# ScalarE's inverse norm placed in front of the first two gelus, with fewer table changes

## The reference, cut to what matters

```python
def attn_layer(x, Wqkv, qs, ksc, Wo):      # 16 heads of 64, windows of 32 tokens
    q, k, v = split(x @ Wqkv)
    q = l2norm(q) * qs
    k = l2norm(k) * ksc
    q, k = rotary(q, scale), rotary(k, 1 / scale)
    return local_attention(q, k, v) @ Wo

def ffn_layer(x, g, bln, W1, b1, W2, b2):  # 128 -> 2 x 341 -> 128
    xn = layernorm(x) * g + bln
    a, gate = split(xn @ W1 + b1)
    return a * gelu(gate) @ W2 + b2

for i in range(6):
    x = attn_layer(shift_tokens(x), ...) + x
    x = ffn_layer(shift_tokens(x), ...) + x
# whole: x += 0.5 * stack(layernorm(x)); x += retention(layernorm(x)); x += 0.5 * stack(layernorm(x))
```

## Time and profile before

| what | value |
|---|---|
| time, median of 3 runs | 3483.53 us (3481.82 to 3486.94) |
| the profiled execution | 3483.61 us |
| its span, first to last instruction | 3481.8 us |
| TensorE busy | 3337.9 us (96%) |
| VectorE busy | 2858.4 us (82%) |
| ScalarE busy | 2433.7 us (70%) |
| GpSimd busy | 2342.3 us (67%) |
| mean granted TensorE clock | 0.985 |

### The profile page before, as it was taken

The page is one execution under the profiler, slowest core; times in us unless marked ns, Lnnn a source line. Parts: engine busy times, 40 slices in busy tenths (PEclk is TensorE's granted clock), DMA queues, the critical chain, the costliest instruction groups (busy, mean ns, idle before and its releaser), DMA issues.

```text
span 3481.8 us, 123144 instructions
## 1 busy us (share of the span) xinstructions
PE 3337.9 (96%) x51660; PEld 1871.0 (54%) x51660; DVE 2858.4 (82%) x6052; ACT 2433.7 (70%) x4133; POOL 2342.3 (67%) x2188
## 2 busy tenths in 40 slices
PE   6999999999999999999788999999999999999996
PEld 3555555555555555555354555555555555555553
DVE  7888888888888888886468888888888888888883
ACT  3677777777777777777425777777777777777775
POOL 5777777777776777775137777777777777677771
PEclk8999999999999999999899999999999999999999
DMA  2001001001001001000100000000010000000000
GB/s 84 12 15 46 12 14 49 12 14 48 12 15 48 12 14 36 10 13 20 39 1 24 14 24 22 17 24 22 12 29 22 12 28 23 12 28 10 12 5 13
DMA packets 49223, 76.64 MB, mean 22 GB/s; under 512 B 7072, under 2 KB 37024, under 8 KB 47136
## 3 DMA queue, kind: packets, MB, share of 16 engines
q1 hardware_dynamic: 48672, 68.76, 6.3%
HBM read 61.39 MB, written 7.34 MB: 20 GB/s over the span
## 4 chain that ended last, share of the span: by engine, by line
PE 51%; POOL 22%; issue 15%; DVE 10%; ACT 1%; POOLq 0%; DMA 0%; SPq 0%; DVEq 0%; ACTq 0%
PE QA L835 10%; PE VS L899 10%; POOL QN L345 8%; POOL QN L352 8%; PE TB L923 6%; PE TB L854 5%; PE VS L949 4%; PE FB L986 4%; POOL Z L361 3%; PE TB L878 3%; DVE T L607 3%; DVE T L602 3%; PE FB L977 3%; PE FB L978 2%; POOL TAB L337 2%
## 5 line engine op out<-in xcount | busy, mean ns | idle before, releaser
L345 POOL TENSOR_TENSOR QN<-T 128x512 f32<-128x512 f32 x768 | 979.4, 1275 | 570.3 <-DVE T L607 551.7
L352 POOL TENSOR_TENSOR QN<-QN,RR 128x512 f32<-128x512 f32 x768 | 792.6, 1042 | 154.4 <-DVE RR L628 154.4
L835 PE MATMUL QA<-WQ,Y 128*128 128x512 f32 x1536 | 753.5, 603 | 23.0 <-DVE T L607 14.7
L899 PE MATMUL VS<-MW,Y 128*32 128x512 f32 x6144 | 738.5, 598 | 6.7 <-DVE Z L694 6.4
L602 DVE TENSOR_TENSOR T<-QA,TAB 128x512 f32<-128x512 f32 x768 | 525.4, 684 | 187.1 <-ACT SQ L452 178.2
L472 ACT ACTIVATE V<-VS 128x512 f32<-128x512 f32 x768 | 455.2, 601 | 251.4 <-PE VS L899 251.2
L923 PEld LDWEIGHTS TB<-CST,QN 128*128 128x128 f32 x3072 | 354.3, 141 | 491.8 <-issue 278.1
L452 ACT ACTIVATE SQ<-QA 128x512 f32<-128x512 f32 x768 | 441.4, 595 | 193.6 <-PE QA L835 182.2
L607 DVE TENSOR_TENSOR T<-QA,TAB 128x256 f32<-128x256 f32 x1536 | 572.4, 414 | 0.0
L361 POOL TENSOR_TENSOR Z<-Z,RC 128x512 f32<-128x512 f32 x384 | 394.4, 1048 | 237.2 <-DVE RC L664 235.1
L923 PE MATMUL TB<-CST,QN 128*128 128x128 f32 x3072 | 483.9, 280 | 34.4 <-DVE Y L634 20.9
(11 more groups left out here) (167 smaller groups left out, 4106.5 us busy)
## 6 DMA issues: line engine op xcount, KB each, us to landing
TAB<-in_tables SPq DMA_DIRECT2D x192, 128.0 KB, 2.1
WQ<-in_w_qk SPq DMA_DIRECT2D x48, 256.0 KB, 3.2
m_dram<-MW SPq DMA_DIRECT2D x6, 1024.0 KB, 5.6
MW<-m_dram SPq DMA_DIRECT2D x6, 1024.0 KB, 5.7
W1R<-in_w SPq DMA_DIRECT2D x12, 341.0 KB, 3.0
WS<-in_w_vt SPq DMA_DIRECT2D x6, 512.0 KB, 5.8
WS<-in_w_out SPq DMA_DIRECT2D x6, 512.0 KB, 5.3
W<-in_w SPq DMA_DIRECT2D x12, 192.0 KB, 2.9
```

The costliest lines, as they stand in the source:

```text
L345: po.tensor_tensor(QN[:, n % 2, k, :], T1[:, k, :], T2[:, k, :], ALU.add).then_inc(s_add, 1)
L352: po.tensor_tensor(heads(QN[:, m % 2, k, :]), heads(QN[:, m % 2, k, :]), RR[:, m % 2, 8 * k:8 * k + 8].unsqueeze(2).to_broadcast([P, 8, DH ...
L835: mm(QA[:, k % 2, :], Y[:, j * P:(j + 1) * P], WQ[:, k, :], start=True, stop=True).then_inc(s_qk, 1)
L899: last = mm(VS[32 * q:32 * q + 32, w % 2, :], Y[:, a:a + WIN], MW[:, l % 2, q, :], start=True, stop=True, tile_position=(0, 32 * q), skip_ ...
```

## The change

ScalarE: in each slot the third eviction of transposed blocks, the logarithm and the exponential move from behind the first and second gelu to the place in front of them. The load of the logarithm's table behind the second gelu is dropped; the third gelu, in the next slot, finds its table loaded. The load behind the first gelu stays. VectorE: in the second-gelu slot the rotation of the fourth block and `inverse_norm` move in front of `hidden`. No other engine's program changes.

```diff
                     nc.scalar.activation(SQF[:, :], FB[:, 0, :], ACT.Square).then_inc(s_fsq, 1)
+                if live(c, 1, it):
+                    qk_out(1, 2)
+                if live(c, 0, it):
+                    ac.wait_ge(s_rm, by_tile(1, n, it, 1))
+                    nc.scalar.activation(LT[:, n % 2, :], NRM[:, n % 2, :], ACT.Ln, scale=LN_SCALE).then_inc(s_rl, 1)
+                    ac.wait_ge(s_rl, by_tile(1, n, it, 1))
+                    nc.scalar.activation(RN[:, n % 2, :], LT[:, n % 2, :], ACT.Exp, scale=-0.5, bias=LNB[:, 0:1])\
+                        .then_inc(s_re, 1)
                 if up0_g is not None:
                     gelu(up0_g, 0)
                     ac.preload_act_table_set("natural_log_exp_and_others")
                 if up1_g is not None:
                     gelu(up1_g, 1)
-                    ac.preload_act_table_set("natural_log_exp_and_others")
-                if live(c, 1, it):
-                    qk_out(1, 2)
-                if live(c, 0, it):
-                    ac.wait_ge(s_rm, by_tile(1, n, it, 1))
-                    nc.scalar.activation(LT[:, n % 2, :], NRM[:, n % 2, :], ACT.Ln, scale=LN_SCALE).then_inc(s_rl, 1)
-                    ac.wait_ge(s_rl, by_tile(1, n, it, 1))
-                    nc.scalar.activation(RN[:, n % 2, :], LT[:, n % 2, :], ACT.Exp, scale=-0.5, bias=LNB[:, 0:1])\
-                        .then_inc(s_re, 1)
                 if live(c, 3, it):
                     p_out(3, 0)
...
                     nc.vector.tensor_tensor(NRM[:, n % 2, :], SSQ[:, n % 2, :], TINY[:, :], ALU.max).then_inc(s_rm, 1)
+                if live(c, 0, it):
+                    rotate(3)
+                    inverse_norm()
                 if up1_g is not None:
                     hidden(up1_g, 1)
-                if live(c, 0, it):
-                    rotate(3)
-                    inverse_norm()
                 if live(c, 2, it):
```

More of the change, by code:

```diff
@@ L527, in slot @@
                     nc.scalar.activation(SQF[:, :], FB[:, 0, :], ACT.Square).then_inc(s_fsq, 1)
-                if up0_g is not None:
-                    gelu(up0_g, 0)
-                    ac.preload_act_table_set("natural_log_exp_and_others")
-                if up1_g is not None:
-                    gelu(up1_g, 1)
-                    ac.preload_act_table_set("natural_log_exp_and_others")
                 if live(c, 1, it):
@@ L541, in slot @@
                         .then_inc(s_re, 1)
+                if up0_g is not None:
+                    gelu(up0_g, 0)
+                    ac.preload_act_table_set("natural_log_exp_and_others")
+                if up1_g is not None:
+                    gelu(up1_g, 1)
                 if live(c, 3, it):
@@ L679, in slot @@
                     nc.vector.tensor_tensor(NRM[:, n % 2, :], SSQ[:, n % 2, :], TINY[:, :], ALU.max).then_inc(s_rm, 1)
-                if up1_g is not None:
-                    hidden(up1_g, 1)
                 if live(c, 0, it):
@@ L684, in slot @@
                     inverse_norm()
+                if up1_g is not None:
+                    hidden(up1_g, 1)
                 if live(c, 2, it):
```

## The result

| kernel | median | range of its runs | ratio to before (95% interval) |
|---|---|---|---|
| before | 3482.82 us | 3477.63 to 3487.06, 20 runs | |
| changed | 3488.47 us | 3485.16 to 3495.87, 20 runs | 1.0017 (1.0010 to 1.0023) |

The change costs 5.65 us (by the interval 3.5 to 8.0 us). The profiled execution of the changed kernel has a span of 3483.6 us. It is one of the quickest of its 20 runs, so the places are read from it and the size is taken from the medians.

The account below looks back on a forecast made before the run. TensorE was taken to bound the kernel, ScalarE's saved 123 us counting nothing; -11.9 us (first-gelu slot) and +18.0 us (second-gelu slot) gave +6.1 us on 3483.61 us, forecast 3490 us, range 3476 to 3497.

Parts of the forecast that it names:

- The bound: First stack's long steady stretch: TensorE busy 1475.34 of 1490.00 us; its 14.7 us idle is all better order could return.
- undisturbed slot: TensorE slot used for comparison: the same work takes 8.37 us against 9.36, so about 0.97 us is lost per group.
- First-gelu slot: Waits for Z and L634 go, P's eviction ends later; loss 0.67 instead of 0.97 us, gain taken as 0.27 a group.
- Second-gelu slot: Gelu and hidden product come later; the third up projection waits 0.46 us plus 0.07, costing 0.53 us a paying group.
- the centre slot: Slot already in the new order: inverse norm's second operation lasts 1.27 us after GpSimd's add; next operation at NRM + 2.81.
- The number of groups that pay: Second-gelu slots: 10 unexplained waits ahead of the scores cover the new wait, so 34 of 44 groups pay.
- the first rival: Waits in the scores don't cover the third up projection; all 44 groups pay, +11.4 us, 3495 us; chance 0.25.
- The sum: Whole kernel: -44 x 0.27 = -11.9 us and +34 x 0.53 = +18.0 us, together +6.1 us.
- The second (no collision): Second-gelu slot: inverse norm gets through before GpSimd's add; wait 0.30 + 0.07 us, +0.7 us, 3484 us; chance 0.14.
- The third: Hidden product never holds TensorE: 3472 us; at the extreme ScalarE's relief removes every loss, 3441 us; chance 0.14, extreme 0.04.
- The fourth rival: P's eviction between second and third gelu might cost table loads; time that of the forecast, sharing its chance of 0.47.
- five signs: 96 fewer loads; L634 wait gone; P transposes at 2.36 us; some 34 up-projection waits; 1.27 us operation in both slots.

Follow-up runs that it names:

- e7: Against the changed kernel: the logarithm's table is loaded behind the second gelu again, so the 96 dropped loads are back; 3488.21 us, ratio to before 1.0013.
- e5: Against e1: in the first-gelu slot P's eviction stands between gelu and table load back; second-gelu slot as before the change; 3441.15 us, ratio to before 0.9874.
- e1: Against the changed kernel: inverse norm ahead of the gelu in the first-gelu slot alone, second-gelu slot as before the change; 3473.47 us, ratio to before 0.9964.
- e2: Against the changed kernel: only the second-gelu slot keeps the change, first-gelu slot as before it; 3501.91 us, ratio to before 1.0051.
- e6: Against the changed kernel: in second-gelu slots GpSimd's add of the fourth rotated block waits until VectorE's inverse norm is through; 3483.70 us, ratio to before 1.0002.
- e4: Against the changed kernel: in the first-gelu slot the eviction of P's first half stands between gelu and table load back; 3458.40 us, ratio to before 0.9927.

## Why the prediction was right, point by point

**The bound.** TensorE's row sets the time, and only its waits count. e7 shows it directly: 96 loads more or less on ScalarE, and no difference. The size that the prediction gave this bound was wrong. It took TensorE's idle time, 14.7 us in the long stretch, as all that a better order could return. Between the first and the last third up projection of the first stack's steady groups the kernel before takes 1409.40 us with 13.40 us of idle time, and e5 does the same work in 1387.93 us (185.97 to 1573.90), 21.47 us less. The window of the kernel before, then e5's two rows:

```profile
189.10:1598.50 1409.40, 1396.00 (x22423) 784.82 (x22422) 1206.11 (x2596) 1042.01 (x1770) 1007.24 (x945) 1.00 0.08 23
...
185.97 1.02 PE L984 MATMUL FB<-XN,W 128*85 128x512 f32 x2
...
1573.90 1.02 PE L984 MATMUL FB<-XN,W 128*85 128x512 f32 x2
```

The busy time, with its modelled ends of matmuls, covers part of the losses: the transposes of P at 844.40 come 0.18 us late and no idle time is booked before them. The prediction's comparison with an undisturbed slot found what the busy share hides.

**First-gelu slot.** Forecast: the waits for Z and L634 go, P's eviction ends 4.51 us after NRM, the P transposes start 2.36 us after the projections, and the slot gains 0.27 us. In the trace the transposes start 2.39 us after them and the gain is 0.27 us; e1 prices it alone at 12.5 us (by the interval 8 to 17) against 11.9 forecast.

**Second-gelu slot.** Forecast: hidden product at NRM + 2.81 us, a wait of 0.46 us and 0.07 us behind it. The trace has 2.81, 0.46 and 0.07 us, and e2 shows the slot alone at 18 us. The step that carried this was the reading of the centre slot as the order that the change would make. The Trainium skill, page "SBUF — State Buffer", section "Who interferes with whom", has the rule behind it, that a VectorE instruction with two inputs in SBUF and a GpSimd instruction that reads SBUF lock each other out, the later one in full; e6, which moves only GpSimd's add, agrees, with 0.19 us instead of 1.27.

**The number of groups that pay.** Forecast 34 of 44, from 10 unexplained waits ahead of the scores in the kernel before. In the profile after 36 pay. The ten do lie where the prediction took them to lie: in the trace before, the scores ahead of the third up projection take 1.74 to 2.33 us from the first start to the last in ten of the 44 groups, and 1.27 us in the others. The 8 groups that don't pay in the profile after are eight of the same ten, with scores of 1.69 to 2.06 us, as here, where the up projection follows its projection by 0.86 us without a wait:

```profile
1329.24 0.33 PE L948 MATMUL VS<-KT,QT 64*32 64x64 f32 x11 [0.30 <-issue]
...
1329.99 1.02 PE L834 MATMUL QA<-WQ,Y 128*128 128x512 f32 x2
1330.85 1.02 PE L976 MATMUL FB<-XN,W 128*85 128x512 f32 x2
```

The traces of e2, e4 and e7, with the same order in this slot, have 36, 36 and 38 paying groups (42, 42 and 44 waits less the six of the tails). So the first rival (all 44 pay, 3495 us) is out in all four executions that were traced. What makes these waits was not tried and stays open.

**The sum.** By the trace it is -44 x 0.27 + 36 x 0.53 = +7.2 us; 6.1 was forecast, and 5.65 (3.5 to 8.0) is measured. The difference of the two prices can be read directly, from one third up projection to the next in two groups whose scores are not drawn out: 66.73 us before and 66.99 us in the changed kernel, 0.26 us more.

```profile
255.84 1.02 PE L977 MATMUL FB<-XN,W 128*85 128x512 f32 x2
...
322.57 1.02 PE L977 MATMUL FB<-XN,W 128*85 128x512 f32 x2
...
253.77 1.09 PE L976 MATMUL FB<-XN,W 128*85 128x512 f32 x2 [0.29 <-DVE HB L640]
...
320.76 1.09 PE L976 MATMUL FB<-XN,W 128*85 128x512 f32 x2 [0.30 <-DVE HB L640]
```

So the mechanism and both prices were right, and the number of paying groups was two too low. The measured interval can't tell 6.1 from 7.2; that the forecast lies nearer to 5.65 than the trace's own sum is luck. The two profiled executions differ by 1.8 us only (3481.8 and 3483.6 us of span), and no reading here rests on that difference.

**The rivals.** The second (no collision) is what e6 built: before's time, as it said. The third had the right reach and the wrong reason: 43 us were to be had, not from ScalarE's freed time but from two places of its order, and e5 has them with no load dropped. The fourth rival's doubt is settled by the copy at 858.20, which runs under the gelu's table in 0.59 us with no load.

**What would show it.** Of the five signs named there, the dropped loads, the vanished wait for the residual add, the late transposes of P and the long second operation in both slots (1.26 us from 840.75 in the first-gelu slot) are in the trace as described. The up projection's wait is there 36 times instead of some 34, with 0.30 us of idle time instead of 0.4; from start to start the delay is the 0.46 us forecast. P's eviction ends 4.53 us after NRM (839.35 to 843.88), against the forecast 4.51, and the steady stretches have no new regular wait besides these two. NRM and the eviction:

```profile
839.16 0.19 DVE L678 TENSOR_TENSOR NRM<-SSQ,TINY 128x32 f32<-128x32 f32 x1
...
843.28 0.60 ACT L478 ACTIVATE PT<-TB 128x512 f32<-128x512 f32 x1
```

## What to carry to other kernels

Time saved on an engine that does not set the end is worth what it does to the order: here 96 dropped table loads gave nothing, while one copy moved ahead of one load gave some 30 us. When an edit swaps the order on one engine, look in the same trace for a slot that already has the new order, and take its durations, collisions included. And split an edit by the places where it acts before judging it: a gain of 12 us and a loss of 18 us looked like no change.

## What the runs showed of the hardware

A copy under the gelu's table takes no load of its own. No row of the trace before showed that; in e4, e5 and the changed kernel the copy runs there in 0.59 us (830.93 in e5), as elsewhere. And a table load costs little beyond its own 1.28 us: in e5 it starts 0.02 us after the copy's end (831.52 to 831.54), and in e7 the gelu starts 0.02 us after the load's end (863.96 to 863.98).
